# Graph layer on one Trainium2 core: the one-hot products of the second stage cut into column halves

## The reference

```
w    = silu(edge_scalars @ Wfc1) @ Wfc2                 # per edge, 192 weights
e0,e1 = (x0 @ Wl1_0, x1 @ Wl1_1) * a, gathered by edge_src
mid0..mid3 = products of w, e0, e1 and the edge's sh    # per edge
n_k  = segment_sum(mid_k, edge_dst) / max(count, 1)     # mean per node
out_s, out_v = n @ Wl2_s, n @ Wl2_v ; alpha = n @ Wa
out  = layernorm(x + x @ Wsc + alpha * conv(out_s, out_v))
```

## Time and profile before

| | |
|---|---|
| median of three runs | 930.89 us |
| profiled execution | 931.75 us, of which the span of the trace is 930.0 us |
| granted TensorE clock, mean | 0.989 |
| busy share of the span | PE 93%, PE weight loads 79%, VectorE 87%, ScalarE 68%, GpSimd 77% |
| second stage | from about 555 us of the span to its end |

### The profile page before, as it was taken

One profiled execution on the slowest core, in us unless ns is written; L12 is line 12 of the kernel. 1 busy time (PEld: TensorE's weight loads), 2 busy tenths in 40 slices (PEclk: granted clock), 3 DMA queues, 4 the chain that ended last, 5 costly groups with the idle time before them and its releaser, 6 DMA issues.

```text
span 930.0 us, 32660 instructions
## 1 busy us (share of the span) xinstructions
PE 867.5 (93%) x10688; PEld 731.0 (79%) x10688; DVE 811.5 (87%) x2797; ACT 635.4 (68%) x1961; POOL 714.2 (77%) x804
## 2 busy tenths in 40 slices
PE   3999999999998999999999989999999999999995
PEld 2778788788887878888888778888888787888884
DVE  3789999999988999999999878888889888988887
ACT  2456555565554655656555547898999898998897
POOL 6777777777777776777777316888999898998895
PEclk9999999999999999999999999999999999999998
DMA  6455544454464555456544217999999999999993
GB/s 181 117 165 169 165 140 132 131 141 131 131 134 135 178 156 143 137 149 185 149 142 129 84 74 201 305 305 303 305 305 314 300 313 310 307 309 301 303 308 144
DMA packets 87540, 186.77 MB, mean 201 GB/s; under 512 B 17647, under 2 KB 48139, under 8 KB 87372
## 3 DMA queue, kind: packets, MB, share of 16 engines
q1 hardware_dynamic: 48411, 87.72, 29.2%
q10 hardware_dynamic: 20016, 61.15, 19.6%
q0 software_dynamic: 18944, 35.81, 16.9%
HBM read 119.66 MB, written 64.95 MB: 199 GB/s over the span
## 4 chain that ended last, share of the span: by engine, by line
PE 36%; POOL 26%; issue 19%; DVE 11%; DMA 5%; ACT 1%; POOLq 0%; ACTq 0%; DVEq 0%
POOL res L640 9%; POOL gat L587 7%; PE ps L736 7%; POOL xa L628 6%; PE ps L715 5%; PE ps L733 4%; PE ps L696 4%; PE ps L702 4%; DVE mid L984 3%; POOL xa L624 3%; PE ps L795 3%; PE ps L678 3%; DVE z L1002 2%; DMA out<-fin 2%; PE ps L676 2%
## 5 line engine op out<-in xcount | busy, mean ns | idle before, releaser
L587 POOL DMA_INDIRECT gat<-turned,srcs x196 | 191.5, 977 | 66.9 <-issue 61.9
L587 POOL DMA_INDIRECT gat<-spread,srcs x196 | 188.6, 962 | 61.8 <-issue 59.7
L795 PE MATMUL ps<-win,hot 60*128 60x162 f32 x2352 | 190.5, 308 | 0.7 <-DVE hot L1325 0.7
L862 ACT ACTIVATE e_sb<-ps 128x512 f32<-128x512 f32 x196 | 106.4, 595 | 123.6 <-PE ps L702 122.1
L736 PE MATMUL ps<-wy,mid 128*128 128x161 f32 x784 | 183.0, 315 | 0.0
L795 PEld LDWEIGHTS ps<-win,hot 60*128 60x128 f32 x2352 | 166.4, 188 | 17.0 <-issue 14.4
L1008 DVE SCALAR_TENSOR_TENSOR msg<-ps,sha,z 128x161 f32<-128x161 f32 x392 | 151.0, 385 | 13.9
L640 POOL TENSOR_TENSOR res<-agg,pre 128x640 f32<-128x640 f32 x98 | 151.8, 1549 | 10.4 <-ACT agg L907 10.4
L733 PE MATMUL ps<-wy,mid 128*128 128x97 f32 x784 | 142.2, 263 | 0.2 <-DVE mid L984 0.2
L984 DVE TENSOR_TENSOR mid<-ps,e_sb 128x512 f32<-128x512 f32 x196 | 133.1, 679 | 2.9 <-PE ps L715 2.9
L907 ACT ACTIVATE agg<-ps,coef 128x160 f32<-128x160 f32 x392 | 122.2, 398 | 18.5 <-DVE coef L1365 15.2
(11 more groups left out here) (104 smaller groups left out, 1495.7 us busy)
## 6 DMA issues: line engine op xcount, KB each, us to landing
win<-rows SPq DMA_DIRECT2D x392, 114.6 KB, 3.7
rows<-msg SPq DMA_DIRECT2D x98, 326.0 KB
out<-fin ACTq DMA_DIRECT2D x47, 640.0 KB, 6.0
xin<-x_g ACTq DMA_DIRECT2D x92, 322.0 KB, 4.8
gat<-turned,srcs POOLq DMA_INDIRECT x196
gat<-spread,srcs POOLq DMA_INDIRECT x196
eas<-ea_t SPq DMA_DIRECT2D x7, 384.0 KB, 4.6
xin<-x_g SPq DMA_DIRECT2D x6, 322.0 KB, 3.4
```

The lines of the kernel that those rows point to most:

```text
L587: pool.indirect_dma_start(out=gat[:, slot, first:first + of.shape[1]], out_offset=None, in_=of, in_offset=bass.IndirectOffsetOnAxis(ap=src ...
L795: last = nc.tensor.matmul(agg_ps[b1][:, 2 * h + k, 0:SW], hot[side(h), b1, k, c, :], win[side(h), (b - 1) % RING, k, c, 0:SW], start=c == ...
```

## The change

Each product of 60 edge slots by 128 nodes becomes two of 60 by 64 nodes, on the two column halves of the array. With the two row halves, four products then lie on the four quarters of the array. A group has 24 products in place of 12, in the order column half, then row half; operands, accumulation and the semaphore after the last one stay. The products of x that follow already use the quarters.

```diff
                     for k in range(2):
                         for c in range(WC_ROWS):
-                            for h in range(2):
-                                last = nc.tensor.matmul(
-                                    agg_ps[b1][:, 2 * h + k, 0:SW], hot[side(h), b1, k, c, :],
-                                    win[side(h), (b - 1) % RING, k, c, 0:SW],
-                                    start=c == 0, stop=c == WC_ROWS - 1)
+                            for n in range(2):
+
+                                nodes = slice(n * HALF, (n + 1) * HALF)
+                                for h in range(2):
+                                    last = nc.tensor.matmul(
+                                        agg_ps[b1][nodes, 2 * h + k, 0:SW],
+                                        hot[side(h), b1, k, c, nodes],
+                                        win[side(h), (b - 1) % RING, k, c, 0:SW],
+                                        start=c == 0, stop=c == WC_ROWS - 1)
                     last.then_inc(agg_done, 1)
```

## The result

The changed kernel takes 944.91 us (median of 4 runs, 943.63 to 952.46), the kernel before beside it 931.07. The ratio is 1.0188 [1.0151, 1.0225]: slower, by 13.8 us between the medians and by 17.5 us by the ratio, where the forecast said 929.7 and a range up to 936.5. The profiled execution took 944.01 us, 942.3 of it the span.

The account below looks back on a forecast made before the run. A loop through PE, VectorE and GpSimd, 7.11 us a pair, was taken as the bound, with window waits from DMA. Terms from -2.4 to +4.5 us, taken as -1.2, gave 929.7 us against the median; range 921 to 936.5.

Parts of the forecast that it names:

- The products: Sums on PE: each of twelve slots holds four records and stays at 0.14 us, upper bound 0.15.
- the weight loads: Ahead of the sums: 64-column loads take 134 ns, not 186; the first gets 0.05 us shorter, the others stay hidden.
- the tile shape: Between sums and quarters of x: one shape removes the 0.08 us pause and hides L811's first load, 0.05 us.
- rival 3: Sums on PE: column halves take turns, slots of 0.28 us, stage 122 us longer, 1053 us; chance 0.04.
- rival 4: Between sums and quarters of x: the pause stays, same total of 929.7 us; chance 0.66 together with the forecast.
- The loop: Through PE, VectorE and GpSimd: a pair of steps goes from 7.11 to 7.06 us, 2.4 us over 49 pairs.
- GpSimd alone takes 3.45 us: Second stage: GpSimd's own step when `fin` doesn't wait, a floor below the loop that steady steps would not undercut.
- rival 1: Second stage: PE sets the pace; 913 us if all counted, 920.5 with GpSimd's floor, half 925.5; chance 0.18.
- Instructions: ... 0.3% of DMA time, up to 1.1 us: Instruction fetching: 48 more records a group take 0.3% of DMA time, costing up to 1.1 us over some 370 us.
- Rival 2: VectorE's window waits (L1317): windows come late more often, 937.5 us at half as much again, 944 at twice; chance 0.12.

Follow-up runs that it names:

- wide products of x: Changed kernel with the 16 quarter products of x a group made 4, each four times as wide, 48 records less, output wrong in these: 926.59 us, 0.9961.
- the last kernel shown: Changed kernel with GpSimd making `xa` one step earlier, so that the transposes don't wait for it: 950.06 us, 1.0232.
- the change's second run: Changed kernel once more, unaltered, timed beside the kernel before and the runs with half of each output store left out: 943.37 us, 1.0118.
- the shortened quarters: Changed kernel with three of the four x products a group left out (48 records), output wrong in these: 928.52 us, 0.9958.

## Why the prediction was wrong

*The products, the weight loads, the tile shape*: right. Slots of 0.14 us with four records on the quarters (rival 3 is out), loads at 133 ns, no pause ahead of x (rival 4 is out), 1.71 us foreseen as 1.73. The Trainium skill, in "TensorEngine Tiling (Array Packing)", section "Restrictions and Gotchas", excludes Fast Weight Load under column tiling; the trace shows no loss from that, 186 - 133 = 53 ns for the 64 columns fewer.

*The loop*: right as a mechanism, its gain too large. The first load's 0.05 us should have gone from the pair; 0.02 did. On the row, the sums of 48 records last 1.89 us where 24 lasted 1.93: only 0.04 sooner at the end. With the records of before, the change and wide products of x together win a little: 0.9961 [0.9939, 0.9983], 3.6 us, against 2.4 of the loop and 1.2 forecast. No run has the wide products with the sums in halves, so what the sums' shape has of that stays open.

*GpSimd alone takes 3.45 us*: wrong, though it moved no term of the sum; rival 1's 920.5 us rested on it. With `fin` not waiting, it goes on from 710.12 after 706.78 us in the last kernel shown, 3.34 us:

```profile
706.78 0.48 POOL L650 TENSOR_SCALAR fin<-res,rstd,shift 128x160 f32<-128x160 f32 x1 [0.73 <-DVE shift L1364]
...
710.12 0.47 POOL L650 TENSOR_SCALAR fin<-res,rstd,shift 128x160 f32<-128x160 f32 x1
```

*"Instructions: ... 0.3% of DMA time, up to 1.1 us"*: this is the step that failed. It priced the added records by the share of DMA time that their fetches take, and that share was right (1.0% became 1.2%). The records cost about 18 us (944.91 - 926.59, the same work in 48 records less; 15 to 21 by the ratios of both runs of the change). Two things were missing. TensorE itself can run out of instructions, for the time that a packet takes to come and not for its bytes: 8.0 us of pauses in 300. And windows land later: 20.8 - 8.3 = 12.5 us more of waits than with fewer records, though only 17.0 - 13.1 = 3.9 between the change's second run and the shortened quarters. The two rows add up to 20.3 us in 300. In the same 300 us the change gets through 77.7 groups and the wide products through 81.6, which is 14 us of lost time, so the rows are not to be added without care.

How much of the second is due to the fetches' bytes and how much to PE's own pauses stays open. Twenty copies of as many bytes in before cost some 4 us, so bytes alone are not it, but those copies were not in packets of 16 KB; the rest is a difference, not a measurement, and no run adds records without adding work.

*Rival 2* came true in its price (twice the waits, 944 us) and not in its reason; that the time agrees is luck. It let VectorE come sooner to windows that had not landed. VectorE comes as soon with wide products of x, and waits 8.3 us.

*Rival 1* is out: PE's own step (3.45 us with halves and 3.26 with quarters, both with `xa` early) sets no pace while the loop stands. The Trainium skill, in "TensorEngine Tiling (Array Packing)", section "PSUM Bottleneck", says that tiling speeds up TensorE but not the emptying of PSUM, which may then bind. The trace agrees as far as PE's step lost 0.19 us and the pair 0.02 (7.11 to 7.09, 7.06 forecast); that it is PSUM's emptying that holds the pair is not shown, since the loop goes through GpSimd as well.

## What to carry to other kernels

Count the instruction records of an engine as a resource of their own: a product split in two for a better shape doubles its records, and where the DMA engines are nearly full, that can cost several times what the shape gives. Look for idle time "issue" inside a block of independent instructions, and beside it for a packet on the instruction queue some 2 us earlier. Then count the engine's records up to the end of each pause: where the counts are a multiple of a packet's records apart (256 here), the engine had run out of instructions. And follow a loop before speeding up a stage of it: making `xa` earlier won more than any tiling here.

## What the runs showed of the hardware

- TensorE's records come over q8 in packets of 16 KB, 256 records each (27,159 in 106). Twelve of the change's 13 pauses ended 2.2 to 2.7 us behind a packet's start, and all 13 at one place of a packet's content.
- GpSimd's records come over another queue, q14, in packets of 8 KB: 4,704 more took it from 82 to 118 packets.
- Register instructions are not small change: six in a row become one record of 74 ns, and 48 such records a group made the kernel 1.4079 times as long on PE and 1.175 times on GpSimd; over 98 groups that is some 81 and 35 ns a record.
- A change of tile shape in the middle of the sums made the pair of steps 7.30 us, 0.19 longer than with either shape throughout (7.11, 7.09 or 7.10).
